# A Fourier-attention and FFN kernel on eight cores: weight-preparation loads go from the GpSimd queue to the SyncE queue, at another pace

## The reference

```python
xn = layernorm(x)                                   # x: [32, 2048, 1024]
q, k, v = [(xn @ W + b) split into 16 heads of 64]  # Wq, Wk, Wv
q_freq, k_freq, v_freq = rfft over the 2048 positions   # 1025 frequencies
idx = top_k(abs(q_freq).mean(-1), 64)               # per batch and head
attn = softmax((q_top.real * k_top.real).sum(-1) / (8 + 1e-8))
out_freq = q_mean_freq everywhere, attn * v_top.real at idx
attn_out = irfft(out_freq) @ Wo + bo
h = silu(xn @ wg.T) * (xn @ wu.T)                   # int32 weights / 127, hidden 3072
return x + attn_out + h @ wd.T
```

## Time and profile before

| what | us |
|---|---|
| median of 3 executions | 5936.88 (5803.94, 6002.89, 5936.88) |
| the profiled execution, its own time | 5808.28 |
| its span on the slowest core (core 0) | 5806.7 |
| spans of the eight cores | 5768.8 to 5806.7 |
| TensorE busy | 4710.7 (81%) |
| VectorE, ScalarE, GpSimd busy | 1367.9, 836.4, 30.5 |

### The profile page before, as it was taken

How to read it: one execution, slowest core, us unless ns; L and a number is a source line. 1 busy time by engine, 2 the same in 40 slices (tenths; PEclk the granted TensorE clock), 3 DMA queues, 4 the chain that set the end, 5 groups by cost and what they waited for, 6 DMA issues and landing times.

```text
span 5806.7 us, 51940 instructions; the slowest of 8 cores (5768.8 to 5806.7 us)
## 1 busy us (share of the span) xinstructions
PE 4710.7 (81%) x20322; PEld 1992.3 (34%) x20720; DVE 1367.9 (24%) x1819; ACT 836.4 (14%) x976; POOL 30.5 (1%) x60
## 2 busy tenths in 40 slices
PE   0745578899875998799894798889986599889989
PEld 0212232344332433234342333334433243324434
DVE  2211122022223322212122333202222332211212
ACT  2111111122001111022101111112200111112210
POOL 0000000000000000000000000000000000000000
PEclk9967788999987999899996899889998799989999
DMA  4123412132330311122342211222233131212234
GB/s 130 36 76 109 115 40 61 63 90 73 125 114 29 73 44 44 61 80 77 93 133 73 54 42 44 58 69 84 77 123 112 33 69 44 63 47 84 77 104 122
DMA packets 574296, 441.88 MB, mean 76 GB/s; under 512 B 276940, under 2 KB 473676, under 8 KB 574056
## 3 DMA queue, kind: packets, MB, share of 16 engines
q1 hardware_dynamic: 556776, 375.60, 23.1%
q0 software_dynamic: 8064, 29.36, 1.8%
q10 hardware_dynamic: 9216, 33.56, 1.4%
HBM read 373.46 MB, written 65.01 MB: 76 GB/s over the span
## 4 chain that ended last, share of the span: by engine, by line
PE 78%; DMA 11%; DVE 6%; issue 3%; ACT 1%; DVEq 0%; SPq 0%; ACTq 0%
PE pw L614 15%; PE pw L946 12%; PE pw L955 11%; PE pw L987 11%; PE pw L494 9%; PE pw L856 4%; PE pw L568 4%; PE pw L889 4%; DMA strm<-dft_cos 2%; DMA strm<-wq_s 2%; PE pw L502 1%; DMA strm<-wv_s 1%; DMA r<-wdT_s 1%; PE pw L660 1%; DMA r<-x 1%
## 5 line engine op out<-in xcount | busy, mean ns | idle before, releaser
L614 PE MATMUL pw<-r,strm 128*128 128x512 bf16 x4012 | 935.5, 395 | 293.7 <-DMA strm<-dft_cos 240.6
L946 PE MATMUL pw<-r,strm 128*128 128x512 bf16 x3012 | 698.4, 382 | 38.0 <-ACT strm L930 34.9
L955 PE MATMUL pw<-r,strm 128*128 128x512 bf16 x3012 | 689.9, 379 | 3.2
L614 PEld LDWEIGHTS pw<-r,strm 128*128 128x128 bf16 x4096 | 411.6, 101 | 816.0 <-issue 369.0
L494 PE MATMUL pw<-strm,r 128*128 128x512 bf16 x2250 | 540.8, 390 | 72.4 <-DMA strm<-wv_s 40.9
L987 PE MATMUL pw<-r 128*128 128x512 bf16 x1992 | 456.7, 383 | 65.8 <-DMA r<-wdT_s 62.1
L965 DVE TENSOR_TENSOR r<-strm,pw 128x1024 bf16<-128x1024 bf16 x192 | 234.5, 1221 | 1036.8 <-PE pw L955 1036.8
L946 PEld LDWEIGHTS pw<-r,strm 128*128 128x128 bf16 x3072 | 302.3, 98 | 404.7 <-issue 48.0
L955 PEld LDWEIGHTS pw<-r,strm 128*128 128x128 bf16 x3072 | 300.6, 98 | 362.4
L494 PEld LDWEIGHTS pw<-strm,r 128*128 128x128 bf16 x2304 | 215.3, 99 | 389.3 <-issue 164.0
L962 ACT ACTIVATE strm<-pw 128x1024 bf16<-128x1024 f32 x192 | 196.6, 1024 | 1015.5 <-PE pw L946 1015.4
(11 more groups left out here) (168 smaller groups left out, 2577.5 us busy)
## 6 DMA issues: line engine op xcount, KB each, us to landing
strm<-dft_cos SPq DMA_DIRECT2D x96, 512.0 KB
r<-x SPq DMA_DIRECT2D x64, 512.0 KB
spA<-wg SPq DMA_DIRECT2D x48, 512.0 KB
spC<-wu SPq DMA_DIRECT2D x48, 512.0 KB
spB<-wg SPq DMA_DIRECT2D x48, 512.0 KB
spD<-wu SPq DMA_DIRECT2D x48, 512.0 KB
strm<-dft_sinn SPq DMA_DIRECT2D x32, 512.0 KB
r<-crt SPq DMA_DIRECT2D x8, 2048.0 KB
```

The source lines that it names most:

```text
L614: e.matmul(pw[pwi][:, eta * 512:(eta + 1) * 512], slotv[:, tau, :], sig[:, tau, eta * 512:(eta + 1) * 512], start=(tau == 0), stop=(tau == ...
L946: e.matmul(pw[pg][:, tq * 512:(tq + 1) * 512], wgv[:, dc, :], xnT[:, dc, th * 1024 + tq * 512:th * 1024 + (tq + 1) * 512], start=(dc == 0) ...
L955: e.matmul(pw[pu][:, tq * 512:(tq + 1) * 512], wuv[:, dc, :], xnT[:, dc, th * 1024 + tq * 512:th * 1024 + (tq + 1) * 512], start=(dc == 0) ...
```

## The change

It moves the loads of all 56 preparation items from GpSimd to SyncE, and spreads the items otherwise: the query DFT serves 2 items a block instead of 3, the key DFT 1 instead of 2, and the value projection, which served none, 1 a tile. `Wo` joins the pending list after the query DFT. The last flush stands behind the value projection instead of ahead of the read-back of its weights. The casts and stores stay what they are.

```diff
-        em("g", lambda e, it=it, src_ap=src_ap:
+        em("q", lambda e, it=it, src_ap=src_ap:
            e.dma_start(out=it, in_=src_ap), writes=SP4[par], dma=True)
...
-            if b == 0 and si == 1:
+            if b == 0 and si >= 1:
                 prep_service(1)
...
             if b == 0:
-                prep_service(3 if si == 0 else 2)
+                prep_service(2 if si == 0 else 1)
...
             prep_attn_pend("Wk")
             prep_attn_pend("Wv")
-            prep_attn_pend("Wo")
         else:
             phase_ln_proj(b)
         phase_fft(b, 0)
         prefetch_wbuf(b, 1)
         if b == 0:
+            prep_attn_pend("Wo")
             prep_pending.extend((src, dst, tk, True) for (src, dst, tk) in ffn_chunks)
         phase_proj(b, 1)
         phase_fft(b, 1)
+        prefetch_wbuf(b, 2)
+        phase_proj(b, 2)
         if b == 0:
             prep_service(99)
             prep_flush()
-        prefetch_wbuf(b, 2)
-        phase_proj(b, 2)
```

## The result

The changed kernel is 0.5% slower: the ratio of its executions to those of the kernel before is 1.0051, 95% interval 1.0038 to 1.0065, some 30 us. Its median is 5833.6 us over 9 executions. Those of before that are left stand at 5800 to 5814 us, those of the changed kernel at 5832 to 5847.

The account below looks back on a forecast made before the run. Batch 0 was taken as bound by SP's queue, which waits for each landing. Terms of 15.7 - 14.4 - 1.6 + 23.1 + 24.6 - 8.7 + 1.2 = 39.9 us on 5808.3 gave 5848 us, range 5815 to 6043.

Parts of the forecast that it names:

- the term of the start: Start of the kernel: nothing covers the eight Wq loads, x loads start at 92.7 us instead of 77.07, +15.7 us.
- First DFT: Query DFT of batch 0: two services a block instead of three, period 38.4 us instead of 40.2, -14.4 us in all.
- that of the key projection: Key projection of batch 0: 16 services of 6.05 us take 96.8 against 71.0 and delay the cosine slice, +23.1 us.
- those of the two DFTs: Batch 0: query DFT -14.4 us with two services a block; key DFT +24.6 us with every slice waiting.
- loads nearly free on SP: Rival for batch 0: SP's loads cost only their 0.33 us issue, sum -36.8 us, 5771 us; chance 0.08.
- everything on SP is dear: Rival for SP's queue: load plus store takes 8.1 us or more instead of 6.05, 5927 us; chance 0.12.
- The third, a key DFT without longer stalls: Rival for the key DFT: stores hidden, blocks run at 7 to 9 us, -45 instead of +24.6, 5779 us; chance 0.03.

Follow-up runs that it names:

- queue-alone kernel: The kernel before with the 56 loads moved to SP and the old pace and order kept; ratio 1.0117 against the kernel before.
- the one that doesn't wait: Changed kernel without SP's landing wait for the 48 loads behind Wq's, each issued behind an older item's store; 5848 and 5851 us, no ratio.
- the services in the projections: Changed kernel with loads on POOL and all 48 items behind Wq's served in batch 0's three projections, none in a DFT; ratio 0.9605 against the kernel before.

## Which steps of the prediction failed, and what of it held

What failed first is the last step, from the sum to the forecast: "The profiled execution took 5808.3 us (span 5806.7), so **5848 us**", with "a change of 40 us holds for all of them alike" and "It would read as no clear change". The sum says 39.9 us slower. But it is put on one profiled execution, and the time of before that the reader has is the median of 5936.88. Beside that, 5848 us is 1.5% faster, so the number forecasts a gain and the sum a loss. Like set beside like, 5832 to 5847 us against 5800 to 5814, the change is a loss of 0.5%, and it does not read as "no clear change": the interval of 1.0038 to 1.0065 tells it from nothing, far inside the 2% that the prediction took for the limit. A forecast of this size is one of a ratio or of a difference.

In the sum itself the term of the start was mis-sized: "the queue is free at 21.66 + 1.4 = 23.1 us", +15.7 us, measured +10.9. The step took the time of the constants from the kernel before, where POOL's loads ran beside them. I had freed the weight slices and stores of those loads and forgotten the eight small transfers ahead. The first load left at 18.36, and the run with Wq's loads on POOL put the last of the small ones back to 22.13.

First DFT, "period 30.15 + 8.25 = 38.4": measured 37.7, and -17.1 in all for -14.4. From a slice to the first store it is 29.7 us (287.46 to 317.16) for 30.15, and store, load, store take 8.0 for 8.25. The lead of a slice, taken at 4.65 us, was 4.4 to 5.2 us in its eight blocks, 4.7 in the mean, and is not the reason.

The mechanism held step by step: SP waits for each landing, so a load that nothing covers is added at its full length, a load under matmuls costs nothing, and a service costs TensorE what stands between it and the next slice. The signs of all terms are as forecast; that of the key projection is within 0.4 us, those of the two DFTs within 2.7. Nearly all stages came out shorter than forecast, so the misses add up and don't cancel: 39.9 us forecast, 29.6 measured from the start to the `Wo` slices, and 4.8 of the difference are the start's.

The rivals: loads nearly free on SP is out, by the queue-alone kernel (+23.1 us in the key projection) and by the one that doesn't wait (-12). The Trainium skill ("Trainium Kernel Development and Optimization", Key Constraints) says that issuing from several engines only saves issue time. That does not describe a program whose sequencer waits for each landing: here the second queue was worth 0.6 to 1.2% (1.0117 against 1, 1.0051 against 0.9992, 0.9768 against 0.9685). That everything on SP is dear is out too: a service took 5.9 us in the key projection and not 8.1, stores 2.07 us and loads 3.7, less than beside POOL. The third, a key DFT without longer stalls, is out by the rows of 19.3 and 21.7 us a block.

## What to carry to other kernels

Where an issuing engine waits for each transfer to land, count its queue like an engine's busy time: lengths add up, and a stage is as long as the longer of the queue and the work. More important than the queue was the order on it: a store that waits for this block's result must not stand ahead of the next block's input. Moving that one line was worth 2.7% here, and giving the service work to the stages that had an idle queue 4%, while a change of queue and pace moved a half per cent.

## What the runs showed of the hardware

A transfer on one queue is slowed by transfers of another queue on the same core, small ones too. At the start SP waits 22.1 us in sum for the landing of eight stores of 256 KB beside POOL's loads, the longest 4.3 us, and 13.4 us without them, the longest 1.7. The eight small constant loads ahead of them are through later as well: the last is issued at 16.90 us alone and at 21.66 and 22.13 us beside POOL's. I had expected only the large ones to share.

Two transfers of one queue, 512 KB and 256 KB, issued 0.42 us apart, took 4.85 us together in the mean, against 5.9 one behind the other: overlapping them saved 1.05 us, and not the 2.07 of the shorter one.

A stalled TensorE also works slower. The DFT matmuls of the query DFT on core 0, in the changed kernel and with the services in the projections, where the engine runs through (the columns are those of the earlier trace rows, without the other engines):

```profile
241.10:513.30 272.20, 126.51 (x502) 53.31 (x512) 0.73 0.28 75
231.20:358.80 127.60, 112.00 (x502) 50.38 (x512) 0.96 0.39 91
```

The same 502 recorded matmuls are busy 126.51 us at a granted clock of 0.73 and 112.00 at 0.96, the means of stretches at the two levels of 1.2 and 2.4 GHz. So of the 136 us by which TensorE's time in this DFT fell, 14.5 go with the clock, and the rest is waits that went.
